# Windowed attention in a fused block: the tail of a step run in the next step, and stacks repeated by their reads

## The reference, cut to what matters

```
for i in range(0, S, w2):                    # windows of 64 tokens, one every 32
    start, end = max(0, i - w4), min(S, i + window_size - w4)
    attn = softmax(einsum('bqd,bkd->bqk', q[:, start:end] * scale, k[:, start:end]))
    wo = einsum('bqk,bkd->bqd', attn, v[:, start:end])
    # the overlap with the window before is blended by a linear ramp, the rest is set
out = ctx @ wproj + bproj + residual
```

## Time and profile before

| what | value |
|---|---|
| runs, median (lowest to highest) | 343.5 us (335.82 to 345.52) |
| profiled execution | 340.69 us |
| its span, first to last instruction | 338.9 us |
| mean granted TensorE clock, share of 2.4 GHz | 0.832 |
| TensorE busy with matmuls | 284.3 us, 84% |
| VectorE busy | 224.2 us, 66% |
| ScalarE busy | 141.1 us, 42% |
| GpSimd busy | 75.3 us, 22% |
| moved by DMA | 23.71 MB |

### The profile page before, as it was taken

One profiled execution on the slowest core, in us unless ns is written; L12 is line 12 of the kernel. 1 busy time (PEld: TensorE's weight loads), 2 busy tenths in 40 slices (PEclk: granted clock), 3 DMA queues, 4 the chain that ended last, 5 costly groups with the idle time before them and its releaser, 6 DMA issues.

```text
span 338.9 us, 10357 instructions
## 1 busy us (share of the span) xinstructions
PE 284.3 (84%) x4168; PEld 223.3 (66%) x4168; DVE 224.2 (66%) x634; ACT 141.1 (42%) x282; POOL 75.3 (22%) x116
## 2 busy tenths in 40 slices
PE   4865479599897988969998899887899989999992
PEld 2323356387775766747876787565697779778992
DVE  7554764466758376452645626498857898798986
ACT  1343136328354462734226235654536216624220
POOL 5453240311403141000101010215540024003020
PEclk9775558859789796995558557999989999999999
DMA  6107752377617365271710340000000000101011
GB/s 183 43 0 202 167 120 47 106 164 174 172 35 177 92 122 150 52 186 35 142 22 6 120 143 3 0 2 0 0 2 1 0 2 0 32 2 31 2 32 32
DMA packets 21902, 23.71 MB, mean 70 GB/s; under 512 B 3296, under 2 KB 18528, under 8 KB 21856
## 3 DMA queue, kind: packets, MB, share of 16 engines
q1 hardware_dynamic: 21856, 23.06, 27.2%
HBM read 14.67 MB, written 8.13 MB: 67 GB/s over the span
## 4 chain that ended last, share of the span: by engine, by line
PE 47%; DVE 17%; issue 9%; SPq 8%; DMA 8%; ACT 7%; POOL 2%; ACTq 0%; DVEq 0%; POOLq 0%
PE bank L655 6%; SPq L285 5%; PE bank L407 5%; PE bank L450 4%; DMA qst<-mt 4%; PE bank L371 4%; PE bank L430 3%; PE bank L392 3%; DVE xh L1032 3%; PE bank L440 3%; PE bank L637 3%; PE bank L639 3%; PE bank L638 3%; DVE acc L1371 2%; DMA vmsk<-in_vmask 2%
## 5 line engine op out<-in xcount | busy, mean ns | idle before, releaser
L1073 DVE TENSOR_REDUCE nm<-bank 128x8 f32<-128x512 f32 x64 | 43.6, 688 | 28.3 <-PE bank L392 28.2
L878 POOL TENSOR_TENSOR rs<-ve,mhalf 128x2 f32<-128x2 f32 (+1 forms) x24 | 19.4, 810 | 137.4 <-DVE ve L1029 130.6
L740 ACT ACTIVATE prob<-bank 128x512 f32<-128x512 f32 x64 | 36.6, 600 | 29.1 <-PE bank L407 28.6
L392 PE MATMUL bank<-kst,qst 48*64 48x64 bf16 x1024 | 32.5, 213 | 6.4 <-issue 4.3
L830 ACT ACTIVATE sg<-bank 128x512 f32<-128x512 f32 x32 | 18.9, 601 | 43.5 <-PE bank L639 42.0
L655 PEld LDWEIGHTS bank<-wds,hh 128*128 128x128 f32 x256 | 32.3, 191 | 7.0 <-issue 5.4
L655 PE MATMUL bank<-wds,hh 128*128 128x128 f32 x256 | 33.7, 277 | 2.8 <-DVE acc L1371 2.3
L392 PEld LDWEIGHTS bank<-kst,qst 48*64 48x64 bf16 x1024 | 25.4, 125 | 16.0 <-issue 13.3
L407 PE MATMUL bank<-qst,kst 50*64 50x64 bf16 x1024 | 31.0, 213 | 3.9 <-DMA qst<-mt 3.5
L430 PE MATMUL bank<-prob,vb 128*32 128x64 f32 x1024 | 27.8, 258 | 7.6 <-issue 4.7
L1371 DVE SCALAR_TENSOR_TENSOR acc<-bank,rt,acc 128x128 f32<-128x128 f32 x112 | 32.6, 341 | 1.2
(11 more groups left out here) (140 smaller groups left out, 498.8 us busy)
## 6 DMA issues: line engine op xcount, KB each, us to landing
qst<-stack_scratch SPq DMA_DIRECT2D x32, 216.0 KB, 4.8
stack_scratch<-parts SPq DMA_DIRECT2D x16, 216.0 KB, 2.5
kst<-stack_scratch SPq DMA_DIRECT2D x16, 216.0 KB, 5.0
stack_scratch<-parts SPq DMA_DIRECT2D x16, 144.0 KB, 2.4
stack_scratch<-parts SPq DMA_DIRECT2D x16, 72.0 KB, 2.1
qst<-mt SPq DMA_DIRECT2D x64, 4.0 KB
out_x<-fin SPq DMA_DIRECT2D x4, 256.0 KB, 2.3
xs<-in_x SPq DMA_DIRECT2D x1, 896.0 KB, 7.2
```

The lines of the kernel that those rows point to most:

```text
L392: m = pe.matmul(psa[g % 2][WIN * half:WIN * half + WIN, WIN * h2:WIN * h2 + WIN], qst[n][eo][rows_, h2, at:at + WIN], kst[n][rows_, h2, at ...
L740: act.activation(prob[g // 2 % 2][:, :, g % 2, :], psb[g % 2][:].rearrange("p (h q) -> p h q", h=H2), ACT.Exp).then_inc(exp_done, 1)
L1073: dve.tensor_reduce(nm[:, g, :], psa[g % 2][:].rearrange("p (h k) -> p h k", h=H2), AX_X, ALU.max, negate=True).then_inc(max_done, 1)
```

## The change

Six edits are made together.

1. `write_parts` is one transfer of the three parts of queries and keys, each once; the scratch is half as large. `read_stacks` issues 12 transfers, which repeat a part by reading it three, two or one times. It no longer reads `qst[n][1]`.
2. ScalarE makes `qst[n][1]` from `qst[n][0]` in two copies for each sequence (`copy_odd`), and `scores_a(b, 4)` waits for both.
3. `gather_context`, the copy of the context, `project_out` and `attention_out` of sequence b run in step b + 1, in the middle of its first half.
4. `project_v` is done one sequence later than before, in step b for b + 1; `copy_v` follows.
5. `project_qk(b + 3)` moves behind `scores_a(b + 1, 5)`; `copy_qk(b + 3)` becomes the last entry of ScalarE's step, behind `exp(b + 1, 1)`, and `cut_qk(b + 3)` the last of VectorE's step, ahead of the next step's `copy_mt(b + 1, 1)`. SyncE's order in a step becomes `write_mrow(b, 1)`, `write_parts(b + 2)`, `write_mrow(b + 1, 0)`, `read_stacks(b + 2)`.
6. `keep_busy` has six matmuls in a step where it had nine, and none in the last step.

The core of the diff:

```diff
@@ sync
-                for t0, n, k, src in ((0, 3, 0, parts[:, 0:1, 0, :].broadcast_to([P, 3, LINE])),
...
+                sp.dma_start(scr[b].rearrange("t k p n -> p (t k) n"), parts[:].rearrange("p t k n -> p (t k) n")
+                             ).then_inc(written, 16)
...
+                for k, stack, runs in ((0, qst[n][0], ((0, 0, 3), (3, 1, 2), (5, 2, 1))),
+                                       (1, kst[n], ((0, None, 3), (3, None, 2), (5, None, 1)))):
                     for r in range(2):
+                        for at, part, count in runs:
+                            rows_of = scr[b].rearrange("t k (d h) n -> t k d h n", h=NH)[:, k, :, H2 * r:H2 * r + H2, :]
+                            src = (rows_of[0:count] if part is None else
+                                   rows_of[part:part + 1].broadcast_to([count, HD, H2, LINE]))
+                            first_row = 64 * r + HD * at
+                            sp.dma_start(stack[first_row:first_row + HD * count],
+                                         src.rearrange("t d h n -> t d (h n)")).then_inc(stack_ready, 16)
...
             def step(b):
                 write_mrow(b, 1)
-                if b == 0:
-                    write_parts(2)
-                elif b + 2 < B:
-                    read_stacks(b + 2)
+                if b + 2 < B:
+                    write_parts(b + 2)
                 if b + 1 < B:
                     write_mrow(b + 1, 0)
-                if b == 0:
-                    read_stacks(2)
-                if b + 3 < B:
-                    write_parts(b + 3)
+                if b + 2 < B:
+                    read_stacks(b + 2)
@@ tensor, step(b)
                 probs_v(b, 0)
                 scores_b(b, 3)
                 a(0)
-                keep_busy(2)
+                if b + 2 < B:
+                    pe.wait_ge(qk_ready, after(qk_ready, 4 * (b + 3)))
+                if b:
+                    gather_context(b - 1)
+                if ahead:
+                    project_v(b + 1, 0)
+                    project_v(b + 1, 1)
...
                 a(1)
+                probs_v(b, 1)
+                if b:
+                    project_out(b - 1)
+                scores_b(b, 4)
+                a(2)
+                scores_b(b, 5)
+                a(3)
+                turn_sums(b, 0)
+                if ahead:
+                    keep_busy(3)
...
                 a(5)
+                if prep:
+                    pe.wait_ge(mt_ready, after(mt_ready, 2 * b + 3))
+                    project_qk(b + 3)
                 scores_b(b, 7)
...
                 turn_sums(b, 1)
-                keep_busy(5)
-                gather_context(b)
                 if ahead:
+                    keep_busy(3)
                     scores_b(b + 1, 1)
@@ scalar
+            def copy_odd(b, half):
+
+                act.wait_ge(stack_ready, after(stack_ready, 192 * (b + 1)))
+                heads = slice(H2 // 2 * half, H2 // 2 * (half + 1))
+                even, odd = [qst[b % DEEP][eo][0:64 + ROWS, heads, LINE - S:LINE] for eo in range(2)]
+                act.activation(odd, even, ACT.Copy).then_inc(odd_ready, 1)
...
                 exp(b, 2)
+                if b:
+                    copy_ctxt(b - 1)
                 exp(b, 3)
...
                 copy_pv(b, 0)
+                if ahead:
+                    copy_odd(b + 1, 0)
+                exp(b, 4)
+                if ahead:
+                    copy_v(b + 1)
+                    copy_odd(b + 1, 1)
+                exp(b, 5)
                 if prep:
+                    copy_xt(b + 3)
...
                     exp(b + 1, 1)
-                if b + 2 < B:
-                    copy_v(b + 2)
+                if prep:
+                    copy_qk(b + 3)
@@ vector, step(b)
                 maxima_next(1)
+                if b:
+                    attention_out(b - 1)
...
                 normalise(b, 1)
                 if norm:
                     ln_d(b + 4)
-                attention_out(b)
...
+                if prep:
+                    cut_qk(b + 3, 0)
+                    cut_qk(b + 3, 1)
```

More of the change, by code:

```diff
@@ L195, in build @@
         parts_step = sem("parts_step")
-        q_written, k_written = sem("q_written"), sem("k_written")
+        written = sem("written")
         stack_ready = sem("stack_ready")
+        odd_ready = sem("odd_ready")
         v_done, v_ready = sem("v_done"), sem("v_ready")
@@ L300, in _ @@
             write_parts(0)
-            sp.wait_ge(ones_ready, after(ones_ready, 2 * DEEP))
+            sp.wait_ge(ones_ready, after(ones_ready, 3 * DEEP))
             read_stacks(0)
@@ L386, in scores_a @@
                     pe.wait_ge(max_done, after(max_done, 8 * b + g - 1))
+                if g == 4:
+                    pe.wait_ge(odd_ready, after(odd_ready, 2 * (b + 1)))
                 par, halves = spans(g)
@@ L397, in scores_b @@
             def scores_b(b, g):
-                pe.wait_ge(mrow_ready, after(mrow_ready, 128 * b + 64 * (g // 4 + 1)))
+                if g % 4 == 0:
+                    pe.wait_ge(mrow_ready, after(mrow_ready, 128 * b + 64 * (g // 4 + 1)))
                 if g:
@@ L523, in _ @@
                 scores_a(0, g)
+            keep_busy(6)
+            scores_b(0, 0)
+            scores_b(0, 1)
             pe.wait_ge(mt_ready, after(mt_ready, 1))
             project_qk(2)
[L526 to L531, removed]
             def step(b):
-                ahead, prep, values = b + 1 < B, b + 3 < B, b + 2 < B
+                ahead, prep = b + 1 < B, b + 3 < B
                 def a(g):
@@ L550, in step @@
                     transpose_x(b + 3)
[L551 to L562, removed]
                 a(4)
+                pe.wait_ge(att_ready, after(att_ready, b))
                 if ahead:
[L565 to L568, removed]
                     transpose_m(b + 1, 0, w1b)
@@ L589, in step @@
                     first(0, 0)
+                a(7)
+                turn_sums(b, 1)
                 if ahead:
-                    pe.wait_ge(mt_ready, after(mt_ready, 2 * b + 3))
+                    keep_busy(3)
+                    scores_b(b + 1, 1)
                 else:
                     first(0, 1)
-                    pe.wait_ge(att_ready, after(att_ready, b))
-                a(7)
-                turn_sums(b, 1)
-                keep_busy(5)
-                gather_context(b)
-                if ahead:
-                    scores_b(b + 1, 1)
-                else:
-                    first(0, 2)
-                project_out(b)
             for b in range(B):
                 step(b)
+            gather_context(B - 1)
+            first(0, 2)
+            project_out(B - 1)
             def second(g, c):
@@ L713, in copy_qk @@
                 act.wait_ge(parts_step, after(parts_step, 3 * b))
-                act.wait_ge(q_written, after(q_written, 48 * b))
-                act.wait_ge(k_written, after(k_written, 48 * b))
+                act.wait_ge(written, after(written, 16 * b))
                 act.activation(qk[:, 0, :], w0b[:, 0:LINE], ACT.Identity, bias=bqs[:], scale=SCALE
@@ L772, in _ @@
             copy_v(0)
+            copy_odd(0, 0)
+            copy_odd(0, 1)
             copy_xt(2)
-            copy_qk(2)
-            copy_v(1)
             exp(0, 0)
             exp(0, 1)
+            copy_qk(2)
             def step(b):
@@ L787, in step @@
                 copy_pv(b, 0)
+                if ahead:
[5 more added lines that the diff above has]
+                exp(b, 5)
                 if prep:
-                    copy_qk(b + 3)
-                exp(b, 4)
-                exp(b, 5)
+                    copy_xt(b + 3)
                 if not ahead:
@@ L1198, in step @@
                 maxima_next(1)
+                if b:
+                    attention_out(b - 1)
                 if norm:
                     ln_a(b + 4)
+                if group is not None:
+                    ln2_stats(group)
                 maxima_next(2)
@@ L1204, in step @@
                 maxima_next(3)
-                if group is not None:
-                    ln2_stats(group)
                 normalise(b, 0)
@@ L1226, in step @@
                     ln_d(b + 4)
-                attention_out(b)
-                if not ahead:
-                    ln2_stats(NG - 1)
+                if prep:
+                    cut_qk(b + 3, 0)
+                    cut_qk(b + 3, 1)
             for b in range(B):
                 step(b)
+            attention_out(B - 1)
+            ln2_stats(NG - 1)
             normed_tokens(NG - 1)
```

56 lines of the change are left out of this document (19 added, 37 removed).

## The result

The changed kernel takes 405.67 us (median of 4 runs, 403.54 to 406.01), against 341.24 us for the kernel before in the same runs: a ratio of 1.201, with a 95% interval of 1.189 to 1.213. The ratios here leave out the runs that are over 1.5% above the fastest of their own kernel, so that they can differ by a per cent or so from the quotient of two medians. I had forecast 344 us and a range of 331 to 357. The profiled execution spans 404.2 us, 65 more than before.

The account below looks back on a forecast made before the run. A step was taken to be bounded by TensorE's hand-written order, its clock and few long loops through other engines. Terms +7.5, -1.8, -0.5 and -1.5 summed to +3.7 on the profiled 340.7: 344 us, range 331 to 357.

Parts of the forecast that it names:

- The reads against a rule: Last stack read before the next `scores_a(., 0)`: lands in 2.1 us, nothing waits; with 4.8, 2.2 us a step, 11 in all.
- Two of my own signs: In the attention: no wait for the stack reads expected; a granted clock beyond 0.9 or under 0.7 would refute the prediction.
- M(1) to M(5): From the start of step 1's second `copy_mt` to that of step 5's: +7.5 us over four steps.
- The upper bound: Landing of the last stack read: 4.8 us, as for 216 KB reads, costing 2.2 us a step, 11 in all.
- The halved traffic speaks against: Argument at the stack reads, against their landing late: bytes per step fall from 864 + 1296 KB to 432 + 864 KB.
- The rival: Stack reads land late, 2.2 us in each of five steps, giving 355 us; chance 0.08.
- The stall ahead of a(0): TensorE idles some 3.2 us before `scores_a(., 0)` in five steps, waiting for `copy_mt` behind `cut_qk`.
- my own formula: Attention step period: 19.9 us plus 7.4 times the low-clock share; 22.0 us at 28%, against 20.1 before.
- the stall keeps the clock low: Stalls before `scores_a(., 0)` in steps 1 to 5 hold TensorE's clock low: period 24.3 us, 354 us in all; chance 0.27.
- The odd copies: Two ScalarE copies a step, 1.0 us each, 0.95 back to back; `scores_a(., 4)` waits, ending at 9.0 instead of 7.9.
- The tail: Step's end, gather to projection, moves between other matmuls: saves some 0.4 us of gaps a step and three 0.16 us `keep_busy` matmuls.
- The start: Before step 0's second `copy_mt`: one write awaited in place of six, that copy at 54.5 to 55 us; -0.5 us.

Follow-up runs that it names:

- e3: Changed kernel with queries and keys outermost in the scratch, parts written in two transfers, key runs of 24 and 16 rows read at one distance: 382.6 us, ratio 1.116.
- e1: Changed kernel with six writes and four whole stack reads of 48 rows in place of one write and twelve reads: 358.7 us, ratio 1.046.
- e7: Changed kernel with all its transfers, only `cut_qk(b+3)` moved behind the next `copy_mt(b+1, 1)`: 405.2 us, ratio 1.199.
- e4: e1 with `cut_qk(b+3)` moved to the next step, just behind `copy_mt(b+1, 1)`: 341.0 us, ratio 0.996.
- e10: Kernel before with the odd query stack copied on ScalarE and the moved tail together, 48-row transfers kept: 338.7 us, ratio 0.979.
- e9: Kernel before with only the context gather and output projection moved into the next step and five `keep_busy` matmuls dropped: 342.7 us, ratio 0.999.
- e2: e1 with each whole read cut into 24, 16 and 8 rows at one distance, twelve reads: 359.9 us, ratio 1.054.

## Why the prediction was wrong

**The failed step: "The reads against a rule".** I wrote that "a piece of the new last read is 36 KB, so I take 2.1 and nothing waits; with 4.8 it is 2.2 us a step, 11 in all". The last read landed 7.6 us after its issue (119.43) and the issues took up to 0.75 us in place of 0.44, 8 in place of 5.3 us. In the prediction's terms, the landing of the reads stood in the sum at nothing, and it measured 58.3 us of TensorE's waits in seven steps; and the path that bounds a step is the loop through the reads, not the one through `cut_qk`. I priced a read by its bytes and took the landing time from rows of another form, 48 or 128 rows at one distance. Two of my own signs came with it, a wait for the stack reads and a clock under 0.7 (0.69 from M(1) to M(5)). The upper bound was not a bound for reads with outermost counts of 3 and 2. "The halved traffic speaks against" was the wrong argument: bytes fell, and so did the number of engines that carry them. I had not weighed the rule on the number of engines that stands beside e3. The rival had the right place and the wrong price, and 0.08 as its chance.

The forecast's terms beside the profiled executions, as changes against the kernel before, in us:

| stretch | forecast | e1, whole reads | changed kernel |
|---|---|---|---|
| start to M(0) | -0.5 | +0.4 | +7.0 |
| M(0) to M(1) | -1.8 | +0.8 | +7.3 |
| M(1) to M(5) | +7.5 | +15.2 | +36.1 |
| M(5) to the end | -1.5 | +1.9 | +14.9 |
| sum | +3.7 | +18.3 | +65.3 |

The last column less the one before it is what the reads cost, 47 us; the difference of the first two is what else was mis-sized, 14.6 us.

**The stall ahead of a(0).** Its mechanism was right and, in the changed kernel, hidden (e7). By itself it measured 2.3 us where I said 3.2, in six steps where I said five, and its removal was worth 17.6 us (e1 against e4). I had set the period with it at 22.0; e1 shows 23.9. The size that was off is the clock: I took today's share of the low level, 28%, and e1 had 64% (a clock of 0.68). At 64% my own formula, 19.9 + 7.4 x 0.64, gives 24.6. Its 7.4 was never shown in full: the pairs of rows that I named add up to 4.5 to 5.3 over the gather, the values and 16 groups. e10's two steps above, of another order of work, differ by 6.8. So the rival "the stall keeps the clock low", which I gave 0.27, was nearer to the truth than the forecast, even had the reads been whole: 358.7 us is above my range of 331 to 357.

**The odd copies.** I said 1.0 us each, from two rows of other widths. The page of the changed kernel:

```profile
L740 ACT ACTIVATE qst<-qst 112x1024 bf16<-112x1024 bf16 x16 | 16.7, 1052 | 8.8 <-DMA kst<-stack_scratch 8.6
```

1.05 us each, and `scores_a(., 4)` waited for the second 8.1 us in seven steps, 1.2 us a step, where I had 1.1. This part was right.

**The tail.** Some 0.4 us a step and three dummies was the forecast gain. By itself it gained nothing measurable (e9). I named the clock as a rival only for the stall, not for the dummies and gaps that the move takes away.

**The start.** M(0) was to come at 54.5 to 55; it came at 62.26. With whole reads it was 55.68 (e1), so the first twelve reads were slow too.

## What to carry to other kernels

Price a transfer by its access pattern, not by its bytes: write down the outermost count of both sides after the counts that can be joined are joined, and if it is small, expect a few DMA engines at work and a landing several times later; where two such counts stay apart, as in these reads, expect a longer issue too. Two waits before one instruction hide each other, so a stall that was forecast from the order may be real and yet worth nothing until the other is gone. On a list that is close to TensorE's own time, look at the granted clock of each experiment before its waits; seven dummies in idle places came with a clock of 0.88 in place of 0.71, while five at the step's end gave no measurable gain; no run here puts the same number in both places.

## What was not expected of the hardware

- While twelve reads of 864 KB in all are issued, with outermost counts of 3, 2 and 8 in the source, 0.16 to 0.25 of the DMA engines are busy and move 44 to 79 GB/s; the kernel before reached 243 GB/s with 48 rows.
- The issue of a read of the same bytes took 0.36 to 0.37 us or 0.63 to 0.70 us on the average of six, by the form of its source alone (e2 and the changed kernel; e3 shows both forms in one trace).
- A list of matmuls busy for 97% of a stretch can run wholly at 1.2 GHz: e9 was busy for 19.36 of 20.00 us and its granted clock was 0.50.
